# Counting four edge tiles in place of two in each round of a prologue loop, so that two hundred tiles in place of a hundred are scattered there

## What is computed

```python
edge_index = jnp.stack([src, dst])
h = jnp.maximum(_layernorm(x, axis=-1), 0.0)
x = x + _L0_gnn_ref(h, ...)   # relational attention: 8 relations, 4 heads of 64
h = jnp.maximum(_layernorm(x, axis=-1), 0.0)
x = x + _L1_gnn_ref(h, ...)   # graph convolution to 10 clusters, softmax, @ cluster_emb
h = jnp.maximum(_layernorm(x, axis=-1), 0.0)
x = x + _L2_gnn_ref(h, ...)   # edge network + sums over neighbours + three dense layers
h = jnp.maximum(_layernorm(x, axis=-1), 0.0)
x = x + _L3_gnn_ref(h, ...)   # mean over neighbours, two dense layers
return x
```

## Time and profile before

| | before |
|---|---|
| median of 3 runs | 3454.94 us (3450.02 to 3455.64) |
| span of the profiled execution, first to last instruction | 3439.7 us |
| busy: PE / DVE / ACT / POOL | 3044.1 / 1984.0 / 1221.5 / 1011.8 us |
| prologue loop, first to last round | about 147 to 485 us |
| attention stage | about 525 to 1220 us |
| edge stage | about 1220 to 1740 us |

### The profile page before, as it was taken

The page is one execution under the profiler, slowest core; times in us unless marked ns, Lnnn a source line. Parts: engine busy times, 40 slices in busy tenths (PEclk is TensorE's granted clock), DMA queues, the critical chain, the costliest instruction groups (busy, mean ns, idle before and its releaser), DMA issues.

```text
span 3439.7 us, 51402 instructions
## 1 busy us (share of the span) xinstructions
PE 3044.1 (88%) x15820; PEld 1910.6 (56%) x15884; DVE 1984.0 (58%) x5826; ACT 1221.5 (36%) x3509; POOL 1011.8 (29%) x1045
## 2 busy tenths in 40 slices
PE   2788856888888899999997899979999999999998
PEld 1444424555555589999853444445555555545545
DVE  6466665788888877766432543326555555522334
ACT  1122225777777744444320400014444444410000
POOL 2122247777776777777200000000000000000000
PEclk6699987999999999999997799989999999999999
DMA  8845533444433111111166333330000000022232
GB/s 246 323 155 162 167 122 107 108 108 107 108 101 100 31 29 34 34 32 30 29 205 218 94 107 103 91 97 6 6 5 5 6 6 3 23 83 78 80 101 79
DMA packets 247398, 303.39 MB, mean 88 GB/s; under 512 B 122219, under 2 KB 171796, under 8 KB 243092
## 3 DMA queue, kind: packets, MB, share of 16 engines
q1 hardware_dynamic: 194740, 168.58, 17.7%
q0 software_dynamic: 48128, 100.18, 10.0%
q10 hardware_dynamic: 4320, 31.95, 2.3%
HBM read 226.93 MB, written 73.66 MB: 87 GB/s over the span
## 4 chain that ended last, share of the span: by engine, by line
PE 56%; DVE 20%; DMA 8%; issue 7%; DVEq 3%; ACT 3%; POOL 2%; SPq 1%; POOLq 0%
PE PS L1116 16%; PE PS L943 14%; PE PS L929 6%; PE PS L916 6%; DMA SL<-key_d 4%; PE PS L773 4%; DMA BG<-a_d 3%; DVE SUMS L1507 2%; DVE SUMS L1512 2%; PE PS L890 2%; POOL BG L486 2%; DVE BG L1657 2%; DVE OHB L1473 2%; DVEq L1526 2%; ACT SL L687 1%
## 5 line engine op out<-in xcount | busy, mean ns | idle before, releaser
L503 POOL DMA_INDIRECT a_d<-VAL,IDXS x499 | 495.4, 993 | 409.0 <-DVE VAL L1399 220.3
L1116 PE MATMUL PS<-BG,SL 128*128 128x512 f32 (+1 forms) x1440 | 542.6, 533 | 12.0 <-ACT SL L687 12.0
L486 POOL DMA_INDIRECT BG<-feat_d,IDXST x500 | 483.6, 967 | 168.1 <-issue 108.4
L591 ACT ACTIVATE BG<-BG,SL 128x64 f32<-128x64 f32 x2000 | 481.9, 334 | 0.0
L1116 PEld LDWEIGHTS PS<-BG,SL 128*128 128x128 f32 x1440 | 279.7, 197 | 252.4 <-issue 222.2
L526 POOL MEMSET BG<- 128x7680 f32 x1 | 6.5, 6498 | 1371.2 <-DVE MV L1789 1371.2
L890 PE MATMUL PS<-OHB,BG 128*128 128x128 f32 x2000 | 368.5, 309 | 0.0
L890 PEld LDWEIGHTS PS<-OHB,BG 128*128 128x128 f32 x2000 | 270.8, 196 | 115.2 <-issue 115.2
L1507 DVE TENSOR_TENSOR SUMS<-SUMS,PS 128x384 f32 x500 | 275.8, 552 | 62.3 <-PE PS L773 28.9
L929 PE MATMUL PS<-OHB,AL 128*128 128x128 f32 x2000 | 298.9, 278 | 3.8 <-ACT AL L609 2.4
L1594 DVE TENSOR_TENSOR SUMS<-SUMS,PS 128x256 f32 x500 | 210.0, 420 | 156.1 <-PE PS L929 145.4
(11 more groups left out here) (282 smaller groups left out, 4263.8 us busy)
## 6 DMA issues: line engine op xcount, KB each, us to landing
BG<-a_d SPq DMA_DIRECT2D x171, 256.0 KB, 4.1
AL<-a_d SPq DMA_DIRECT2D x137, 256.0 KB, 2.6
a_d<-BG POOLq DMA_DIRECT2D x30, 1088.0 KB, 40.4
feat_d<-SUMS ACTq DMA_DIRECT2D x30, 1040.0 KB, 5.3
BG<-rel_d SPq DMA_DIRECT2D x100, 160.0 KB, 3.4
BG<-in_edge_attr_dram SPq DMA_DIRECT2D x124, 128.0 KB
SUMS<-a_d SPq DMA_DIRECT2D x52, 256.0 KB, 2.6
BG<-feat_d,IDXST POOLq DMA_INDIRECT x500, 2.8
```

Source lines behind the costliest of these rows:

```text
L486: pool.indirect_dma_start(RING[:, t // NB % 3, t % NB, :], None, table, bass.IndirectOffsetOnAxis(ap=IDXST[:, t:t + 1], axis=0),).then_inc ...
L503: pool.indirect_dma_start(a_d.rearrange("n (w o) -> (n w) o", o=1), bass.IndirectOffsetOnAxis(ap=IDXS[:, t:t + 1], axis=0), VAL[:, t:t + 1 ...
L591: last = act.activation(v, v, ACT.Copy, scale=EXT[:, b % 2, k, 1 + q:2 + q])
L1116: last = pe.matmul(PS[:, to + q, 0:width], lhs[:, i, c, :], w[:, c, q * width:(q + 1) * width], start=(c == 0), stop=(c == kc - 1))
```

## The change

A round of the prologue loop now counts four tiles: each half loads 256 keys for each partition in place of 128 and compares twice. SOON is 200 in place of 100, so POOL scatters four tiles a round, and tiles 100 to 199 are no longer turned by PE nor counted by DVE in the attention stage, nor scattered in the edge stage.

```diff
-        SOON = 2 * IT
+        SOON = 4 * IT
...
-        KEYR = SLF[:, 0:2 * P].rearrange("p (i n) -> p i n", i=2)
-        SAME0 = SLF[:, 2 * P:3 * P].bitcast(BF16).rearrange("p (i n) -> p i n", i=2)
+        KEYR = SLF[:, 0:4 * P].rearrange("p (i k n) -> p i k n", i=2, k=2)
+        SAME0 = SLF[:, 4 * P:6 * P].bitcast(BF16).rearrange("p (i k n) -> p i k n", i=2, k=2)
...
-                    load(KEYR[:, h, :], key_d[bass.ds((2 * u + h) * P, P)].partition_broadcast(P), f"key_in{h}")
+                    load(KEYR[:, h, :, :].rearrange("p k n -> p (k n)"), key_d[bass.ds((4 * u + 2 * h) * P, 2 * P)].partition_broadcast(P),
+                         f"key_in{h}")
...
             for t in range(SOON):
-                if t % 2 == 0:
-                    pool.wait_ge(s("val_ready"), t // 2 + 1)
+                if t % 4 == 0:
+                    pool.wait_ge(s("val_ready"), t // 4 + 1)
                 scatter(t)
...
                 dve.wait_ge(s(f"key_in{h}"), 16 * (u + 1))
-                n = bass.ds(2 * u + h, 1)
-                ts(SAME0[:, h, :], KEYR[:, h, :], KEY0[:, n], 0.0, ALU.is_equal, ALU.add, accum_out=MULT0[:, n])
+                for k in range(2):
+                    n = bass.ds(4 * u + 2 * h + k, 1)
+                    ts(SAME0[:, h, k, :], KEYR[:, h, k, :], KEY0[:, n], 0.0, ALU.is_equal, ALU.add, accum_out=MULT0[:, n])
...
-                cp(VAL[:, bass.ds(2 * u, 2)], MULT0[:, bass.ds(2 * u, 2)]).then_inc(s("val_ready"), 1)
+                cp(VAL[:, bass.ds(4 * u, 4)], MULT0[:, bass.ds(4 * u, 4)]).then_inc(s("val_ready"), 1)
```

## The result

The changed kernel is slower: the ratio of its time to that of before is 1.0027, with a 95% interval from 1.0017 to 1.0037, that is +9.3 us (5.9 to 12.8). The medians of 20 runs each are 3455.81 and 3447.76 us. The forecast was slower by 25, 3480.0 us in a range from 3458 to 3498. The median of before rests on 20 runs here and is 7.2 us lower than that of the 3 from which the prediction started, so of the 24.2 us between forecast and measured time 7.2 come from that start and not from the reasoning; the difference of +9.3 is to be set against the +25.1 of the sum.

The account below looks back on a forecast made before the run. The prologue loop was taken as bound by DVE's one-hots and the key loads, attention batches 5 to 9 by DVE. Loop +34.9, gather start +1 and attention -10.8 gave +25.1 on 3454.9: 3480.0 us, range 3458 to 3498.

Parts of the forecast that it names:

- What bounds each stage: Edge stage: PE; prologue loop: the circle of DVE's one-hots and SP's loads; attention batches 5 to 9: DVE's own work.
- batches 5 to 9: Attention stage: without the counts they fall from 135.91 us to the gathers' pace, 125.1, a gain of 10.8 us.
- The start of the gathers: End of the prologue loop: four last scatters leave one gather caught earlier behind DVE's long additions, 1 us, between 0.4 and 1.3.
- What is added on DVE: Prologue loop: a comparison and a register instruction more in each half, 0.84 us a round, floor from 6.1 to 6.95 us.
- term 41.2: Prologue loop: 49 rounds at 0.84 us of added DVE work each, in us.
- a floor gap under 6.7: Prologue loop: shortest rounds were to take 6.9 to 7.0 us; staying under 6.7 would show the prediction wrong.
- The waits for keys: Prologue loop: 33 waits, each 0.29 us longer by the load and 0.42 shorter by the wider window, -4.3 us in all.
- Dilution: Prologue loop: in longer rounds fewer loads meet a table store, waits shrink by 40%, 17 us less, about 3458 us; chance 0.10.
- the middle sum: Whole kernel: loop +34.9, gather start +1, attention stage -10.8, together +25.1 us, a time of 3480.0 us.
- the low one: Whole kernel: the sum with the low bounds, 0.27 us for a half and 0 for the longer load, +5 us, 3460.
- the faster case: Prologue loop: loads are the true limit and the comparisons vanish in their waits, -7 us, time 3446; chance 0.05.
- POOL as the limit: Prologue loop: scatters held back by DVE's one-hots make rounds of 8.1 us, time 3503; chance 0.08, shared with later landings.

Follow-up runs that it names:

- the comparison alone: The kernel before, with a second comparison of the same 128 keys against another column in each half, its count unused: ratio 1.0031, +10.7 us.
- the load alone: The kernel before, with 256 keys loaded for each partition and 128 of them compared: ratio 1.0039, +13.4 us.

## Why the prediction was right in direction and wrong in size

**What bounds each stage** was right: the edge stage took no part (539.3 us in both), the loop's delay went whole into the gathers, and batches 5 to 9 fell to the gathers' pace, 125.4 us against 125.1 forecast. The start of the gathers came out at 0.9 us against 1. The mechanism named, one gather fewer ahead of DVE's long instructions, is there in two traces of three, with 1.3 us each; the third has two gathers ahead and 0.1. That it was four scatters that did it is not shown: the kernel with second buffers and two scatters a round has one gather ahead too.

**The step that failed** is "What is added on DVE", the price of the register instruction: "I take 0.12 plus a few hundredths, 0.42 for a half and 0.84 for a round." It measured 0.56 for a round (6.10 to 6.66), of which 0.54 are the comparisons at 0.27 each; two other steps of the round moved against each other (the row at the loop's top came 0.10 us earlier, one one-hot lasted 0.14 longer), for which I have no cause. The term 41.2 was 27.4. The prediction's own sign of being wrong, a floor gap under 6.7, came true. I had the lower bound right ("hidden") and chose the other end from a row in another stage, where a register instruction stood before an addition from PSUM.

**The waits for keys** were forecast to shrink by 4.3 us in all and those for PE by 2. In the traces the waits for keys grew from a mean of 41.1 to 43.7. The two forces in that term were of the right kind, a later landing against a wider window, and the two single-edit kernels show each, somewhat larger than I put them: 17 us absorbed by the comparison alone (33 x 0.42 = 13.9 and 2 for PE forecast), 13 lost by the load alone (33 x 0.29 = 9.6). With a window wider by only 0.28 and the 0.29 of the landing they cancel. (Of the 33 waits that I counted, 4 lie ahead of the loop's first round; with the 29 inside the term would have been -3.8.)

With 27.4 for 41.2 and 0 for the waits, the sum is 27.4 + 1 - 10.8 = +17.6, near the +15.4 of the spans and still above the timed +9.3 (5.9 to 12.8). So the register instruction accounts for most of the error of the sum, and some 8 us of it stay without a shown cause.

**What stays open.** The dense stage was 5.7 us shorter in the changed kernel, three traces against three, with the same instructions. The granted clock falls there to the lower of its two levels for 3.4 or 6.8 us at a time, while PE is busy for 709 of 738 us, and a round of the stage takes 50.6 us in place of 49.0: in the changed kernel's three traces three, two and three rounds, in before's seven, seven and five. Where the stage begins does not alone decide it. The stage was 742 us in the kernel with the comparison alone (nine such rounds), 731 with the change and second buffers, and 729 with SOON = 0 (one). I have no cause for it. The rest of the difference, the 6 us between the spans and the timed value, is within what three traces on three can tell.

**The rivals.** Dilution (3458 us) comes nearest to the time, but not by its mechanism, since the waits for keys did not shrink. Its arithmetic was loose too: 17 us less than the middle sum of +25 is +8, that is 3463, and less than the low one of +5 it is -12, not 0; and the faster case's own -7 gives 3447.6, not 3446. The faster case and POOL as the limit did not happen; the scatters of the loop still take 0.96 us with four in a round, those beside a one-hot as those beside none.

The prediction named the rule of the Trainium skill on the shared port (SBUF — State Buffer, "SBUF: two separate sides") for VectorE instructions in a two-port mode. The instruction beside the long gather is of another kind: line 1418 is an addition with two inputs in SBUF, which the same section of the Trainium skill names apart, as holding the port only against a GpSimd operation that reads SBUF. The trace agrees with this in that the gather, which takes its row numbers from `IDXST`, lasted 8.59 us beside the 8.16 us addition. For the scatters of 0.96 us beside the 0.38 us one-hots no trace shows a hold.

The Trainium skill's page VectorE: DVE Perf Modes ("The TRN2 errata"), whose estimate of 0.19 us would have given +10, came near to the measured +9.3 by luck: a comparison takes 0.27.

## What to carry to other kernels

Work added to a loop that waits for its own loads costs what the shortest round grows, less what the waits absorb: here 10 us in place of 27 for the comparisons alone. If the same edit makes the loads longer, that can take the relief back (13 us here), so price both edits alone before their sum. Work is worth taking out of a stage only down to the next limit: more than half of what DVE was spared here became idle time behind POOL's gathers. And where a loop's waits for loads are an eighth of its time, as here, try a second buffer before a different share of the work: that edit with its unrolled loop gave 32 us, some 22 of them from the buffers, where the change cost 9.

## What the runs showed of the hardware that I had not expected

A register instruction between two comparisons on VectorE cost nothing: 0.27 us from one comparison to the next, as without it. Before an addition from PSUM it had stood with 0.12 us; which of the differences between the two places matters was not tried.

A jump of the loop on VectorE costs some 0.40 us a round: in the loop unrolled by two, short rounds with and without it take 6.12 and 5.71 us.

Right after the last scatter, a load of another queue stalls. In the changed kernel the last scatter starts at 1554.64, and this is a piece of its chain:

```profile
1555.23 20.13 DMA BG<-in_edge_attr_dram
```

In before the last scatter starts at 1664.89, and the like piece at 1668.77 lasts 17.07 us. It moved with the scatters (by 113.5 us, they by 110.3), it was there in 13 of the 18 traces (16 to 20 us), and PE waited 4 to 8 us for it. The kernel with SOON = 0 has 18 us between the last scatter and its landing at the same place. What holds these transfers was not tried.
